# First feed-forward of a four-stage block: earlier statistics, normalising on ScalarE, integer rounding of the output, first bias by TensorE

## The reference

```python
x = x + tanh(g_xattn[0]) * attention_1head(layernorm(x), ctx)      # 77 keys per batch
x = x + tanh(g_ffn[0])   * ffn0(layernorm(x))
x = x + tanh(g_xattn[1]) * attention_16heads(layernorm(x), ctx)
x = x + tanh(g_ffn[1])   * moe(layernorm(x))                       # 8 experts, top 2, capacity 512

def ffn0(x):                                # w1: 256x1024, w2: 1024x256
    h = float2fix(x @ w1 + b1, 8)           # rounded to multiples of 2**-8
    h = float2fix(pwlin_gelu(h), 8)         # 33 knots, exact gelu at the knots, straight lines between
    return float2fix(h @ w2 + b2, 8)
```

## Time and profile before

| | us |
|---|---|
| median of 3 runs | 590.15 |
| range of the runs | 588.03 to 592.24 |
| the profiled execution's own time | 590.45 |
| its span, first to last instruction | 588.7 |
| outside the span | 1.75 |
| PE / DVE / ACT / POOL busy | 512.1 / 429.6 / 261.0 / 155.8 |
| mean granted TensorE clock | 0.950 of full |

### The profile page before, as it was taken

One profiled execution on the slowest core, in us unless ns is written; L12 is line 12 of the kernel. 1 busy time (PEld: TensorE's weight loads), 2 busy tenths in 40 slices (PEclk: granted clock), 3 DMA queues, 4 the chain that ended last, 5 costly groups with the idle time before them and its releaser, 6 DMA issues.

```text
span 588.7 us, 8396 instructions
## 1 busy us (share of the span) xinstructions
PE 512.1 (87%) x3169; PEld 429.0 (73%) x3169; DVE 429.6 (73%) x782; ACT 261.0 (44%) x381; POOL 155.8 (26%) x126
## 2 busy tenths in 40 slices
PE   7879988877777798989999973599999999999990
PEld 3545656766667787979898851379999999999990
DVE  5577769899898967798987977735748666668340
ACT  1233396766767245555555521033434434443200
POOL 2053200000000013132201212540155273473244
PEclk9989999888899889999999997789999999999996
DMA  6411200000000001121031142120365564572031
GB/s 195 153 36 38 71 1 1 1 1 0 1 1 1 1 1 36 37 72 52 22 103 41 55 152 81 45 63 11 104 152 112 148 142 100 154 153 72 7 35 19
DMA packets 35085, 36.37 MB, mean 62 GB/s; under 512 B 3920, under 2 KB 33893, under 8 KB 34917
## 3 DMA queue, kind: packets, MB, share of 16 engines
q1 hardware_dynamic: 28901, 28.19, 15.2%
q0 software_dynamic: 6144, 7.66, 8.0%
HBM read 28.18 MB, written 8.39 MB: 62 GB/s over the span
## 4 chain that ended last, share of the span: by engine, by line
PE 62%; DVE 22%; issue 7%; ACT 5%; POOL 1%; DMA 1%; DVEq 0%; POOLq 0%; ACTq 0%
PE PS L1239 14%; PE PS L1240 14%; PE PS L1241 14%; PE PS L1558 5%; PE PS L1278 3%; PE PS L1254 3%; PE PS L1503 2%; DVE tmp L918 2%; PE PS L1567 2%; DVE xn L804 2%; DVE hT_lo L937 2%; DVE st L788 2%; DVE tmp L929 2%; PE PS L1367 1%; DVE xT_lo L812 1%
## 5 line engine op out<-in xcount | busy, mean ns | idle before, releaser
L1239 PE MATMUL PS<-w_hi,hT_hi 128*128 128x256 f32 x384 | 115.3, 300 | 25.0 <-DVE hT_lo L937 25.0
L1240 PE MATMUL PS<-w_lo,hT_hi 128*128 128x256 f32 x384 | 113.2, 295 | 0.0
L1241 PE MATMUL PS<-w_hi,hT_lo 128*128 128x256 f32 x384 | 113.1, 295 | 0.0
L1239 PEld LDWEIGHTS PS<-w_hi,hT_hi 128*128 128x128 f32 x384 | 78.5, 204 | 29.7 <-DVE hT_lo L937 28.6
L760 ACT ACTIVATE tmp<-PS,biasT 128x512 f32<-128x512 f32 x64 | 40.6, 686 | 109.6 <-PE PS L1241 109.6
L581 POOL DMA_INDIRECT out<-tmp,dst_idx x32 | 55.7, 1741 | 107.4 <-DVE tmp L1198 100.1
L1239 PE MATMUL PS<-xT_hi,w_hi 128*128 128x512 f32 (+1 forms) x200 | 80.1, 401 | 1.9 <-ACT tmp L657 1.8
L1240 PEld LDWEIGHTS PS<-w_lo,hT_hi 128*128 128x128 f32 x384 | 78.5, 204 | 1.1
L1240 PE MATMUL PS<-xT_lo,w_hi 128*128 128x512 f32 (+1 forms) x200 | 78.4, 392 | 0.0
L1241 PEld LDWEIGHTS PS<-w_hi,hT_lo 128*128 128x128 f32 x384 | 78.3, 204 | 0.0
L1241 PE MATMUL PS<-xT_hi,w_lo 128*128 128x512 f32 (+1 forms) x200 | 78.0, 390 | 0.0
(11 more groups left out here) (210 smaller groups left out, 986.8 us busy)
## 6 DMA issues: line engine op xcount, KB each, us to landing
w_raw<-in_L_ffn_w SPq DMA_DIRECT2D x72, 256.0 KB, 3.2
residual<-in_x SPq DMA_DIRECT2D x4, 512.0 KB, 5.9
out<-residual SPq DMA_DIRECT2D x3, 512.0 KB, 4.2
normed_rows<-xn SPq DMA_DIRECT2D x3, 512.0 KB, 2.9
kv<-in_L_ffn_b SPq DMA_DIRECT2D x1, 1024.0 KB, 5.8
tmp<-in_L_xattn_Wq SPq DMA_DIRECT2D x2, 256.0 KB, 6.9
xn<-normed_rows,src_idx POOLq DMA_INDIRECT x32, 3.1
out<-tmp,dst_idx POOLq DMA_INDIRECT x32, 4.0
```

The lines of the kernel that those rows point to most:

```text
L1239: pe.matmul(o, lh, rh, start=start, stop=False, skip_group_check=skip)
L1240: pe.matmul(o, lh, rl, start=False, stop=False, skip_group_check=skip)
L1241: return pe.matmul(o, ll, rh, start=False, stop=stop, skip_group_check=skip)
```

## The change

Statistics. `mv`, `ve`, `rstd` have 8 slots in place of 2. Rounds 6 and 7 take their statistics in the last iteration of the first attention and just behind it; round 8 in iteration g = 8. GpSimd's list has the same powers in the same order, but before its index constants it now waits for the last residual of the feed-forward (`x2_ready`) too.

Normalising. A new ScalarE function `apply` writes `xn` as scale times x plus a shift, four activations of 128x256 at g % 4 = 0. The shifts (minus mean times rstd) are made on VectorE, by one instruction for rounds 5 to 7 ahead of the first segment, and one for round 8 at g = 10.

Output. `ffn_output` writes 256 (O + b2) to an int32 view, so that the write rounds; `ffn_residual` follows in the same iteration and multiplies by the gate over 256. The separate rounding instruction goes. b2 and the gate are scaled once, ahead of the first segment.

Bias. b1 is loaded again as 8 rows (twice), split in a high part (partitions 0 to 7) and a low part (32 to 39), and each `hidden(g)` starts each of its two 512-column outputs with one matmul of these rows by a matrix of ones and zeros that picks the row. The two bias activations per step go.

```diff
-        N_FIRST, N_LATER = 9, 9
+        N_FIRST, N_LATER = 9, 11
...
+            for row in (0, 32):
+                later(b1_rows[row:row + 8, :], b1_0.rearrange("(r p) -> r p", p=P))
...
+            pool.wait_ge(x2_ready, NC)
...
+            def apply(r):
+                act.wait_ge(shift_ready, 1 if r < 2 * NC else 2)
+                act.wait_ge(tr_ready, r - 1)
+                c = ROUNDS[r][1]
+                if r >= NC + 3:
+                    act.wait_ge(x2_ready, r - NC - 2)
+                for i in range(4):
+                    ins = act.activation(xn[:, r % 2, i, :], xr[:, 4 * c + i, :], ACT.Identity,
+                                         bias=shift_by[:, r % 4, i:i + 1], scale=rstd[:, r % NS, i:i + 1])
+                ins.then_inc(xn_ready, 1)
...
-                for f in range(2):
-                    col = B1_0 + 2 * (g % PAIRS) + f
-                    act.activation(H[:, g % 2, f, :], H[:, g % 2, f, :], ACT.Identity,
-                                   bias=biasT[:, col:col + 1]).then_inc(pre_ready, 1)
-                act.wait_ge(pre_ready, 2 * (g + 1))
...
+                if c == NC - 1:
+                    stats(c + 3)
...
+            dve.tensor_tensor(pick_row, bcast(ident[:, 0:8].unsqueeze(2), [P, 8, P]),
+                              bcast(ident[:, 32:40].unsqueeze(2), [P, 8, P]), ALU.add)
+            dve.tensor_copy(bias_hl[0:8, :], b1_rows[0:8, :])
+            link(dve.tensor_copy(bias_hi[32:40, :], b1_rows[32:40, :]))
+            dve.tensor_tensor(bias_hl[32:40, :], b1_rows[32:40, :], bias_hi[32:40, :].bitcast(F32),
+                              ALU.subtract).then_inc(bias_split, 1)
...
+            stats(NC + 3)
             dve.wait_ge(late_loaded, 48)
+            dve.tensor_scalar(b2_bc[:, :], b2_bc[:, :], 256.0, None, ALU.mult).then_inc(late_split, 1)
+            dve.tensor_scalar(tg_unit, tg[:, 2:3], 2.0 ** -8, None, ALU.mult).then_inc(late_split, 1)
+            dve.wait_ge(late_split, 3)
+            def shifts(r, n):
+                dve.wait_ge(rstd_ready, r + n)
...
+            shifts(NC + 1, 3)
...
-                dve.tensor_tensor(xn[:, (c + 1) % 2, :, :], O, bcast(b2_bc[:, :].unsqueeze(1), [P, 4, D]),
-                                  ALU.add).then_inc(o_free, 1)
+                dve.scalar_tensor_tensor(out=xn[:, (c + 1) % 2, :, :].bitcast(I32), in0=O, scalar=256.0, in1=bcast(b2_bc[:, :].unsqueeze(1), [P, 4, D]),
+                                         op0=ALU.mult, op1=ALU.add).then_inc(o_free, 1)
...
-                link(dve.tensor_scalar(y, y, GRID8, -GRID8, ALU.add, ALU.add))
...
+                        ffn_residual(g // PAIRS - 1)
...
-                if g < NB_PAIRS:
-                    if g % PAIRS == PAIRS - 1 and r + 1 <= 2 * NC:
-                        stats(r + 1)
-                    if g % PAIRS == 0:
-                        apply(r)
-                if PAIRS <= g < NB_PAIRS and g % PAIRS == PAIRS - 1:
-                    ffn_residual(g // PAIRS - 1)
+                if g == 2 * PAIRS:
+                    stats(2 * NC)
+                if g == 2 * PAIRS + 2:
+                    shifts(2 * NC, 1)
...
+                if g == 0:
+                    pe.wait_ge(bias_split, 1)
                 for f in range(2):
+                    if g < NB_PAIRS:
+                        pe.matmul(H[:, g % 2, f, :].rearrange("p (a b) -> p a b", a=4),
+                                  bias_hl, bcast(pick_row[:, 2 * (g % PAIRS) + f, :].unsqueeze(1), [P, 4, P]),
+                                  start=True, stop=False)
```

47 lines of the change are left out of this document (30 added, 17 removed).

## The result

The changed kernel takes 587.53 us (median of 20 runs, 584.63 to 589.48) against 590.8 for the kernel before in the same comparison (20 runs, 587.8 to 592.49). The ratio is 0.9954, with an interval of 0.9939 to 0.9969: faster, by 3.3 us, and not by the 8.8 of the forecast. The sign was right and the size far too large; 587.5 lies above the range of 577.5 to 586.5. The profiled execution took 585.97 with a span of 584.2.

A forecast was written before the change was run, and what follows sets the result against it. Nearly full VectorE and a loop through TensorE were taken to bound the chunks. Savings of 8.1 us up to the last output and 0.65 behind it, 8.8 in all, gave 581.5 us, own range 580 to 583.5, outer range 577.5 to 586.5.

The forecast's parts named there:

- The loop through TensorE: First feed-forward: low_half, project, hidden, grid, segment as second bound; with VectorE it finishes a 30.8 us chunk together.
- VectorE's own sum: First feed-forward chunk: VectorE busy 31.3 of 33.9 us before; the change removes 3.9 us a chunk from it.
- one long gap a chunk: Sign of being right: one TensorE wait of some 3.8 us in each feed-forward chunk, no second above 1.
- The loads: Two small loads more under the semaphore of ScalarE's tanh: up to 1 us covered by idle time, costed at 0.
- the head: Ahead of the chunks: first segment at about 77.5 in place of 74.27, segment 4 at 102.45.
- the level behind the long gap: TensorE's lower clock level in project(4), (8), (12) behind a gap of 3.8: 4.35 us a project, ending at +13.65.
- the end of the tail: After segment 14: L945, the output line before, at +28.3 (30.4 before), then 2.5 to the next stats (3.19 before).
- Stats of round 6 lies in a wait of VectorE of 1.20, so 0.8 of its 1.92 remains: Last attention chunk: moving these statistics there was to cost VectorE 0.8 us.
- About 77.5: Head: time in us at which the segment of step 0 was to come, in place of 74.27.
- the half-gain rival: Loop slow at two places a chunk, hidden(0) at the lower level, or loads sticking out: 585 us, chance 0.21.
- ScalarE's apply: First feed-forward: four 128x256 activations taken at 1.6 us, between 1.24 and 2.5; 2.0 by the skill's page.
- The rival of the upper clock: Gap ahead of project(4), (8), (12) no longer brings the lower level: 2.9 us more gain, 578.7, chance 0.15.

The follow-up runs named there:

- Experiment 4: Changed kernel with the bias part undone: bias back in two ScalarE activations per step, no bias matmuls, splits or extra loads; 591.49 us, ratio 1.0018.
- experiment 8: Kernel before with the bias part alone: two bias matmuls per step on TensorE, none of the bias activations on ScalarE; 588.18 us, ratio 0.9949.
- experiment 1: Changed kernel with the small instruction writing round 6's variance moved behind the last attention residual; 587.22 us, ratio 0.9944.
- experiment 11: Changed kernel with residual behind quantise, bias preparation hoisted, 27 warming matmuls, and softmax scaling ahead of round 6's statistics with variance behind the residual; 576.91 us, ratio 0.979.
- experiment 5: Changed kernel with the picking matrix made in the setup and the bias split in the first attention chunk; 582.18 us, ratio 0.9865.
- experiment 6: Changed kernel with 27 warming matmuls ahead of project(0) in place of 36; 585.05 us, ratio 0.9913.
- experiment 3: Changed kernel with 14 warming matmuls filling TensorE's long gap ahead of project(4), (8) and (12); 583.18 us, ratio 0.9874.
- experiment 7: Kernel before with the integer write alone: output as int32 times 256, no separate rounding instruction; 587.16 us, ratio 0.9947.
- experiment 9: Kernel before with the early statistics and ScalarE's apply alone, bias, rounding and residual's place as before; 590.08 us, ratio 1.0013.
- Experiment 2: Changed kernel with a chunk's feed-forward residual moved from ahead of low_half to behind quantise in its iteration; 581.34 us, ratio 0.9854.
- experiment 10: Changed kernel with the residual behind quantise and the bias preparation hoisted together; 581.01 us, ratio 0.9859.

## Why the forecast came out too large

**The structure held.** The loop through TensorE and VectorE's own sum are nearly equal, so taking 3.9 us off VectorE can't shorten a chunk by 3.9. Chunk 6 to 10 was to be 32.5 and measured 32.47; one long gap a chunk, the waits of VectorE ahead of segments 8 and 12, bias matmuls at steps of 0.23 (0.39 busy), 2.45 from the last output to the next statistics where 2.5 was said. The loads cost nothing: the tanh came 0.49 later (19.54, 19.05 before), inside the idle time that was to cover it, and the activation behind it starts at 20.26 in both profiles. Experiment 4 shows the limit through TensorE: with VectorE relieved and the bias on ScalarE, VectorE waits 3 us ahead of segments 8 and 12 and a chunk takes 33.9 again. The other limit, VectorE's own sum, is less clear, as experiment 8 was profiled in a slow execution.

Three steps failed, all of them terms of the sum that were too small: the head, the level behind the long gap, and the end of the tail.

**The head was undercounted by 2.6.** My steps had segment 0 at 77.5 and segment 4 at 102.45; they came at 79.17 and 105.02.
- "Stats of round 6 lies in a wait of VectorE of 1.20, so 0.8 of its 1.92 remains": the residual came 2.24 later, so 1.4 more. The extra statistics put a `tensor_scalar` under GpSimd's subtraction, and it stood there 1.5 us (experiment 1). Without a `tensor_scalar` at that place the residual comes 0.7 later than before, counted from x_lo (experiment 11), which is my 0.8. The subtraction was in the trace of before too, at 65.12; I had read VectorE's wait and not what ran beside it.
- "About 77.5" was added up wrongly: its terms, less the wait of 2.82 that they fill, give 77.8. That is 0.3.
- From segment 0 to segment 1 it took 4.5 where I took 4.0. VectorE's 1.8 for the matrix and the split of the bias were in the forecast. That hidden(0) waits for them, and with it the grid and ScalarE's table load behind it, I had named only under the half-gain rival; with the hoist the distance is 3.9 (experiment 5).
- ScalarE's apply took 2.07 where I took 1.6, between bounds of 1.24 and 2.5. The Trainium skill ("ScalarE: Activation LUTs", section "What ACT_TABLE_LOAD costs"), by which I had estimated 2.0, was right. My lower bound, half of a 512-wide activation for each, had halved the fixed part too. Here 0.4 on the way from segment 1 to the transposes.

The 36 warming matmuls were in the forecast at their right length. I hadn't worked out when low_half(0) would end, and so not seen that they outlast it by 1.7 us (experiment 6).

**The lower level behind the gap was undersized.** "I let it be slow: +13.65" prices it at one project of 4.35. It took 4.47, 5.28 and 4.38 in the profile. In chunk 10 to 14 project(8) started where it was forecast, 9.3 behind segment 10, and lasted 0.9 longer; with the slow first matmul of hidden(12) that makes 31.9 instead of 30.8, 1.1 us.

**The tail** took 28.8 for 28.3, 0.5. Its slow project was as priced. The 0.5 is at project(14): its 24 matmuls kept the steps of the upper level, but the scores began 3.42 behind its first, not 2.95. What held them the profile doesn't tell.

Together that is 2.6 + 1.1 + 0.5 = 4.2, and 8.8 - 4.2 = 4.6; the profiled executions differ by 590.45 - 585.97 = 4.5. The remaining 1.2 to the gain in the medians, 3.3, is that this execution of the changed kernel was one of its faster ones: its 20 runs span 4.9 us. Where in the kernel the slower ones lose it is open.

**The rival of the upper clock** was priced at 2.9 below the forecast, given with 0.15, and didn't happen in the changed kernel. It is what experiment 3 makes happen, for 4.5 us; of the difference to 2.9, 1.1 is that the level had cost more than 4.35 a project. The half-gain rival, 585 with 0.21, was nearest to the measurement, and one of its mechanisms came, hidden(0) at the lower level; its second slow place in a chunk did not. My chances gave the loop's exact arithmetic too much against a list of small things that can each only cost.

**Where the gain went.** By experiments 7 to 9 the integer write alone is worth 3 us and the bias matmuls alone 2 to 3, the early statistics with the apply nothing. The sum is above what the whole change gives, 3.3, though the intervals (each 1 to 1.5 us either way) are too wide to say by how much. The change has a fourth part, which these three leave out: it moves the residual from the end of iteration 7 to ahead of low_half in iteration 6. Experiment 2 takes that back, with the residual behind quantise in iteration 6, and is 9 us faster than before. The forecast had the residual in its early place, at +6.8, and so had its delay in the sum; that the place could be chosen otherwise I had not asked.

## What to carry to other kernels

When an engine is relieved on a loop that two engines share, look at once at the order of what is left on it: work that nobody waits for (here a residual of 1.2 us) must stand behind what the other engine waits for. That one move was worth 6 us here by itself, twice the change, and next to nothing on top of another edit (experiments 5 and 10), so such gains can't be added up. Before extra instructions are moved under a wait, look at what every other engine does in that stretch, GpSimd too, and count as a cost of its own each matmul whose operand is made late.

## What the runs showed of the hardware

**Idle time of TensorE and the level behind it.** I took all 110 projects of the first feed-forward that start behind an idle time, in the fourteen profiles, and counted from the start of the first to that of the last of their 24 matmuls. That is 2.84 to 2.86 us for a fast one and 3.8 to 5.1 for a slow one, with nothing between. After idle times of up to 1.7 us none of 53 was slow; after 1.9 to 2.9 it was 13 of 26, after 3.2 to 3.6 it was 13 of 16, and after 3.8 or more 15 of 15. The same gap of 3.43 ahead of project(4) was followed by 4.47 in the changed kernel, 5.29 with fewer warming matmuls and 2.98 in experiments 1 and 5. So over these kernels a longer gap was more often followed by the lower level, and between 1.9 and 3.6 us the length alone didn't decide it. What does, these runs don't show: the two profiles of the changed kernel had the same projects to 0.04 us, so it need not be chance from one execution to the next. The level may be part of the spread of one kernel's times, too. Of the changed kernel's runs, the two with a mean granted clock of 0.96 took 586.0 on average and the four with 0.95 took 589.0; but the fastest, 584.63, had 0.955.

**The same in code that no edit touched.** The last attention residual came at 65.60 in the profile of before and at 66.96 in that of experiment 7, with the same instructions ahead of it. The windows from 30 to 45 us, before and then experiment 7, differ mainly in the granted clock, 0.89 and 0.77, and in what it delays.

```profile
30.00:45.00 15.00, 11.49 (x53) 7.34 (x53) 11.50 (x24) 4.58 (x12) 8.36 (x7) 0.89 0.11 35
```

```profile
30.00:45.00 15.00, 11.50 (x47) 7.24 (x45) 11.48 (x24) 3.68 (x12) 7.92 (x6) 0.77 0.12 36
```

A single profile can thus be off by 1.4 us in one place. That is why I compared distances between segments, and why a sum of terms can't be held against one profile more closely than that.

**Ports.** A `tensor_scalar` on four numbers a partition cost up to 1.5 us more beside a full-width GpSimd subtraction, while statistics (1.41), an aggregate (0.38) and a reciprocal (0.18) beside the same subtraction kept their times. GpSimd's small power (1.01 on 128x4) held up nothing that I found: in the kernel before, a `tensor_scalar` at 64.18 kept its 0.23 beside it.
